# Attention and fp8 linear layer on one core: k projected in natural order, mask constants as 32 rows

## What is computed

```python
xn = _layernorm(x, axis=-1)
x = x + attn(xn, q_w, k_w, v_w, o_w, o_b, unity_scale) \
      + ffn(xn, weight_fp8, bias, input_scale, weight_scale)

# attn
allowed = (j % STRIDE == 0) | (jnp.abs(i - j) <= LOCAL)      # STRIDE = 4, LOCAL = 8
q = (x @ q_w) * sigmoid(unity_scale);  k = x @ k_w;  v = x @ v_w     # by heads
scores = jnp.einsum('bhqd,bhkd->bhqk', q, k) / sqrt(D)
attn = softmax(jnp.where(allowed, scores, -jnp.inf))
out = einsum('bhqk,bhkd->bhqd', attn, v) @ o_w + o_b
# ffn
x_dq = clip(x / input_scale, -448, 448).astype(float8_e4m3fn).astype(x.dtype) * input_scale
out = einsum('bsi,oi->bso', x_dq, weight_fp8 * weight_scale) + bias
```

## Time and profile before

| | us |
|---|---|
| median of 3 runs | 1383.69 |
| their range | 1381.85 to 1384.70 |
| profiled execution, its own time | 1381.62 |
| its span | 1379.8 |
| TensorE busy | 1270.9 (92%) |
| VectorE busy | 1019.7 (74%) |
| ScalarE busy | 841.5 (61%) |
| POOL busy | 264.0 (19%) |

### The profile page before, as it was taken

The page is one execution under the profiler, slowest core; times in us unless marked ns, Lnnn a source line. Parts: engine busy times, 40 slices in busy tenths (PEclk is TensorE's granted clock), DMA queues, the critical chain, the costliest instruction groups (busy, mean ns, idle before and its releaser), DMA issues.

```text
span 1379.8 us, 28508 instructions
## 1 busy us (share of the span) xinstructions
PE 1270.9 (92%) x9536; PEld 600.6 (44%) x9536; DVE 1019.7 (74%) x2567; ACT 841.5 (61%) x1540; POOL 264.0 (19%) x381
## 2 busy tenths in 40 slices
PE   5279999954999999999999999999999999999996
PEld 3166767621443433334343433443344334334385
DVE  4299999754887878878887887888788878888232
ACT  2144555411777777777776776777677777777800
POOL 2043333320112111211211122111211121121200
PEclk9689999975999999999999999999999999999999
DMA  3268778962244545354443535354454535442257
GB/s 113 78 183 228 230 219 232 212 192 45 59 106 108 116 107 110 110 112 105 106 114 100 117 100 119 95 121 102 99 116 110 110 99 121 107 107 93 77 192 284
DMA packets 207965, 177.82 MB, mean 129 GB/s; under 512 B 48774, under 2 KB 185046, under 8 KB 206230
## 3 DMA queue, kind: packets, MB, share of 16 engines
q1 hardware_dynamic: 201296, 168.84, 47.9%
q10 hardware_dynamic: 6528, 7.08, 1.6%
HBM read 106.78 MB, written 68.29 MB: 127 GB/s over the span
## 4 chain that ended last, share of the span: by engine, by line
PE 66%; DVE 7%; DMA 3%; issue 1%; ACT 1%; SPq 0%; ACTq 0%; DVEq 0%
PE ps_attend L969 19%; PE ps_attend L954 18%; PE ps_attend L932 15%; DVE masked L900 7%; PE ps_attend L976 5%; PE ps_attend L1062 3%; PE ps_attend L955 3%; PE ps_attend L938 2%; DMA q_op<-q_parts_dram 2%; DMA q_op<-attn_dram 1%; PE ps_attend L929 1%; ACT probs L849 0%; SPq L83 0%; SPq L756 0%; ACT probs L854 0%
## 5 line engine op out<-in xcount | busy, mean ns | idle before, releaser
L900 DVE CUSTOM_DVE_ANT_0 masked<-ps_attend,max_mask 128x620 bf16<-128x620 f32 x1024 | 773.9, 798 | 216.1 <-PE ps_attend L955 208.4
L849 ACT ACTIVATE probs<-ps_attend 128x512 f32<-128x512 f32 x1024 | 563.4, 599 | 212.2 <-PE ps_attend L932 189.8
L954 PE MATMUL ps_attend<-k_op,q_op 96*128 96x512 bf16 x1024 | 398.4, 396 | 35.5 <-DMA q_op<-q_parts_dram 21.1
L932 PE MATMUL ps_attend<-q_op,k_op 99*128 99x512 bf16 x1024 | 309.9, 383 | 10.4 <-issue 9.4
L969 PE MATMUL ps_attend<-probs,v_op 128*32 128x512 f32 x2048 | 275.1, 609 | 0.2 <-ACT probs L849 0.2
L954 PEld LDWEIGHTS ps_attend<-k_op,q_op 96*128 96x128 bf16 x1024 | 99.0, 97 | 331.6 <-DVE peak L900 250.6
L955 PE MATMUL ps_attend<-k_op,q_op 96*128 96x108 bf16 x1024 | 219.3, 214 | 0.0
L730 POOL CAST negmax<-peak 128x16 bf16<-128x16 f32 x64 | 12.6, 196 | 809.2 <-DVE peak L900 809.2
L932 PEld LDWEIGHTS ps_attend<-q_op,k_op 99*128 99x128 bf16 x1024 | 84.7, 98 | 148.9 <-ACT probs L849 49.0
L854 ACT ACTIVATE probs<-ps_attend 108x512 f32<-108x512 f32 x256 | 146.5, 601 | 0.7 <-PE ps_attend L938 0.7
L955 PEld LDWEIGHTS ps_attend<-k_op,q_op 96*128 96x128 bf16 x1024 | 102.0, 100 | 16.6 <-issue 0.8
(11 more groups left out here) (67 smaller groups left out, 969.8 us busy)
## 6 DMA issues: line engine op xcount, KB each, us to landing
k_op<-k_parts_dram SPq DMA_DIRECT2D x96, 256.0 KB, 5.0
q_op<-q_parts_dram SPq DMA_DIRECT2D x384, 64.0 KB, 2.7
v_dram<-v_sb SPq DMA_DIRECT2D x64, 256.0 KB, 3.1
share_rows<-shares_dram SPq DMA_DIRECT2D x64, 256.0 KB
attn_dram<-out_rows SPq DMA_DIRECT2D x64, 256.0 KB, 4.2
v_op<-v_dram SPq DMA_DIRECT2D x48, 288.0 KB
q_parts_dram<-qk_parts SPq DMA_DIRECT2D x48, 256.0 KB, 3.8
k_parts_dram<-qk_parts SPq DMA_DIRECT2D x48, 192.0 KB, 2.3
```

The lines of the kernel that those rows point to most:

```text
L849: ins = nc.scalar.activation(probs[:, r, h], ps_s[st.bank(kind)], ACT.Exp)
L900: nc.vector.tensor_tensor_reduce(masked[:, i % 2], ps_u[i % 2][:, 0:UNIT], keep["max_mask"][:, mask], 1.0, -3e38, ALU.add, ALU.max, peak[: ...
L932: ins = nc.tensor.matmul(bank, k[0:KM, h * S + r * P:h * S + (r + 1) * P], q[0:KM, h], start=True, stop=True)
L954: nc.tensor.matmul(ps_u[i % 2][:, 0:NS], cols, k[0:KR, h * S:h * S + NS], start=True, stop=True)
```

## The change

k is projected in natural order: one matmul of 512 columns in place of one of 128 and one of 384. ScalarE's copy of k and VectorE's first subtraction for k read the bank with a stride and write in the order that attention wants, each as two instructions (`in_order` and `by_stride` give the two views). The constants are 32 rows in DRAM: the three rows of -1 (of zeros on q's side, overwritten by the maxima later) stand ahead of the 29. So POOL's two memsets and their semaphores go, and ScalarE waits at the start of attention until the rows of `q_op` have landed, since it writes maxima over three of them.

```diff
+        def in_order(keys):
+            keys = keys.rearrange("p i (g r) -> p i g r", r=STRIDE)
+            return keys[:, :, :, 0], keys[:, :, :, 1:]
+        def by_stride(keys):
+            ns = CH // STRIDE
+            return keys[:, :, 0:ns], keys[:, :, ns:].rearrange("p i (g r) -> p i g r", r=STRIDE - 1)
...
-            sp.dma_start(keep["k_op"][KM:P], io["near_k"].bitcast(BF16)).then_inc(keep["bands_loaded"], 16)
+            sp.dma_start(keep["k_op"][KR:P], io["near_k"].bitcast(BF16)).then_inc(keep["bands_loaded"], 16)
             for slot in range(QSLOTS):
-                sp.dma_start(keep["q_op"][KM:P, slot], io["near_q"].bitcast(BF16)[:, slot * CH:(slot + 1) * CH].unsqueeze(1)
-                             .broadcast_to([P - KM, HG, CH])).then_inc(keep["bands_loaded"], 16)
+                sp.dma_start(keep["q_op"][KR:P, slot], io["near_q"].bitcast(BF16)[:, slot * CH:(slot + 1) * CH].unsqueeze(1)
+                             .broadcast_to([P - KR, HG, CH])).then_inc(keep["bands_loaded"], 16)
...
-                if isinstance(c, int) and c == 1:
-                    pool.wait_ge(y8_ready, 2)
-                    nc.gpsimd.memset(keep["k_op"][KR:KM], -1.0).then_inc(ones_set, 1)
-                    pool.wait_ge(ones_set, 1)
...
-                    nc.scalar.activation(qk_parts[:, k, 1, 0], ps_k, ACT.Copy).then_inc(hi_ready, 1)
+                    for to, src in zip(by_stride(qk_parts[:, k, 1, 0]), in_order(ps_k)):
+                        last = nc.scalar.activation(to, src, ACT.Copy)
+                    last.then_inc(hi_ready, 1)
...
-                nc.vector.tensor_tensor(rest[:, w], src, qk_parts[:, k, w, 0], ALU.subtract).then_inc(rest_ready, 1)
+                if w == 0:
+                    last = nc.vector.tensor_tensor(rest[:, w], src, qk_parts[:, k, w, 0], ALU.subtract)
+                else:
+                    for to, of, hi in zip(by_stride(rest[:, w]), in_order(src), by_stride(qk_parts[:, k, w, 0])):
+                        last = nc.vector.tensor_tensor(to, of, hi, ALU.subtract)
+                last.then_inc(rest_ready, 1)
...
-                        for cols, keys in ((slice(0, ns), grouped[:, :, :, 0]), (slice(ns, CH), grouped[:, :, :, 1:])):
-                            for i in range(KC):
-                                last = nc.tensor.matmul(ps_k[:, m, cols], wk[:, i, m * P:(m + 1) * P], keys[:, i],
-                                                        start=(i == 0), stop=(i == KC - 1))
+                        for i in range(KC):
+                            last = nc.tensor.matmul(ps_k[:, m], wk[:, i, m * P:(m + 1) * P], xnT[:, k, i],
+                                                    start=(i == 0), stop=(i == KC - 1))
...
             pool.wait_ge(tails_set, 2)
-            nc.gpsimd.memset(k_op[1][KR:KM], -1.0).then_inc(ones_set, 1)
-            pool.wait_ge(ones_set, 1)
...
-            sp.dma_start(k_op[1][KM:P], io["near_k"].bitcast(BF16)).then_inc(keep["bands_loaded"], 16)
+            sp.dma_start(k_op[1][KR:P], io["near_k"].bitcast(BF16)).then_inc(keep["bands_loaded"], 16)
...
+            act.wait_ge(keep["bands_loaded"], 16 * (QSLOTS + 1))
             unrolled(body)
...
-                    if st.n == 1:
-                        pe.wait_ge(ones_set, 1)
```

More of the change, by code:

```diff
@@ L133, in part_project @@
         masks_ready = sem("masks_ready")
-        ones_set = sem("first_ones_set")
         zeros_set = sem("zeros_set")
@@ L504, in body @@
                         pe.wait_ge(rest_ready, 2 * c)
-                    grouped = xnT[:, k].rearrange("p i (g r) -> p i g r", r=STRIDE)
-                    ns = CH // STRIDE
                     for m in range(KC):
-                        for cols, keys in ((slice(0, ns), grouped[:, :, :, 0]), (slice(ns, CH), grouped[:, :, :, 1:])):
-                            for i in range(KC):
-                                last = nc.tensor.matmul(ps_k[:, m, cols], wk[:, i, m * P:(m + 1) * P], keys[:, i],
-                                                        start=(i == 0), stop=(i == KC - 1))
+                        for i in range(KC):
+                            last = nc.tensor.matmul(ps_k[:, m], wk[:, i, m * P:(m + 1) * P], xnT[:, k, i],
+                                                    start=(i == 0), stop=(i == KC - 1))
                     last.then_inc(k_ready, 1)
@@ L659, in part_attend @@
         tails_set = sem("tails_set")
-        ones_set = sem("ones_set")
         q_loaded = keep["q_loaded"]
@@ L1125 @@
     close = np.abs(STRIDE * (place // 3) + 1 + place % 3 - np.arange(S)[:, None]) <= LOCAL
-    near_q = np.where(rows.astype(int) @ close.T.astype(int), np.float32(0), np.float32(-BIG))
-    near_k = np.zeros((P - KM, HG * S + KTAIL), np.float32)
+    near_q = np.zeros((P - KR, S), np.float32)
+    near_q[PARTS:] = np.where(rows.astype(int) @ close.T.astype(int), 0, -BIG)
+    near_k = np.zeros((P - KR, HG * S + KTAIL), np.float32)
+    near_k[:PARTS] = -1
     for h in range(HG):
-        near_k[:, h * S + NS:(h + 1) * S] = rows[:, WPAD:-WPAD]
-        near_k[:, h * S + NS - WPAD:h * S + NS] = 1
+        near_k[PARTS:, h * S + NS:(h + 1) * S] = rows[:, WPAD:-WPAD]
+        near_k[PARTS:, h * S + NS - WPAD:h * S + NS] = 1
     for h in range(HG + 1):
-        near_k[:, h * S:h * S + WPAD] = 1
+        near_k[PARTS:, h * S:h * S + WPAD] = 1
     def bf16_bits(a):
```

## The result

| | before | after |
|---|---|---|
| median (4 runs each, taken together) | 1383.81 | 1351.61 |
| their range | 1381.85 to 1384.70 | 1350.56 to 1354.34 |
| profiled execution, its own time | 1381.62 | 1354.34 |
| its span | 1379.8 | 1352.5 |

The ratio is 0.9772, 95% interval 0.9754 to 0.979: 2.3% faster, 32.2 us where 59.4 were forecast. 1351.61 lies well above the range of 1318 to 1333. The profiled executions differ by 27.3 us; before's was 2.2 under its median, after's the slowest of its four and 2.7 over.

What follows compares the result with a forecast made beforehand. TensorE was taken as busy except in two stalls behind 29-row mask loads on one DMA engine, with an equally long POOL, ScalarE and VectorE loop in projection. 33.2 + 5.5 - 1.0 + 1.0 - 0.3 + 21.0 = 59.4 us gave 1324, range 1318 to 1333.

Steps and rivals of the forecast that it cites:

- whose steps stay as they are: Attention: the gap of 21 us goes and the steps there do not change.
- C: Rival: strided bank reads run at half rate, the cut of k grows 1.1 us in 15 chunks: 1341, chance 0.06.
- D: Rival: strided reads severely slow, at five times the time per element the cut adds 4.5 us x 15: 1392, chance 0.01.
- Mask rows, first place: Start of the kernel: 32 rows spread over sixteen DMA engines, so the third x lands earlier: 33.2 us gained.
- B: Rival: only `k_op`'s long rows spread, `q_op`'s stay on one engine, some 14 us lost: 1338, chance 0.05.
- E: Rival: the change spreads nothing, one DMA engine moves a tenth more: 1384, no change, chance 0.03.
- The memset: Second chunk: without POOL's fill of three rows VectorE's clamp no longer takes 6.18 us: 5.5 us gained.
- POOL's wait for the copy of q: Second chunk: POOL's second operation waits for the copy of q: 1.0 us lost.
- The +1.0 of the long chunk of before: Projection: one chunk of 15.03 us, where TensorE, slow after stalls, made POOL wait, shortens: 1.0 us back.
- Natural order: Projection: TensorE gains 0.97 us per chunk, hidden by another loop; the split cut of k makes chunks 14.03 us: 0.3 us lost.
- A: Rival: TensorE's 0.97 us per chunk counts in full, 14 chunks x 1.0 us: 1310, chance 0.04.
- Mask rows, second place: Start of attention: the first six q loads land earlier behind the mask rows, TensorE's idle time goes: 21.0 us gained.

Runs made afterwards that it cites:

- e3: The changed kernel with k projected, copied and cut as before, so only the 32 mask rows and no POOL memsets: 1328.46 us.
- e5: The changed kernel with TensorE's attention loop aligned to the start of a 256-instruction block: 1328.73 us.
- e8: e5 with the third x loaded ahead of `max_mask` and the mask rows: 1325.74 us.
- e7: e5 with k projected, copied and cut as in the kernel before: 1329.01 us.
- e6: The changed kernel with TensorE's attention loop aligned to slot 216 of its 256-instruction block, 40 instructions left: 1336.40 us.
- e1: The changed kernel with 192 more TensorE instructions, waits for a count long reached, ahead of attention: 1345.99 us.
- e2: The kernel before with 64 more TensorE instructions, waits for a count long reached, ahead of attention: 1407.08 us.

## Why the prediction was wrong

The direction was right. The size was wrong by 27.6 us in the median. One step accounts for most of it: e3 and e5, in which the jumps cost what they cost before, are 23 us faster than the changed kernel. The other 5 us are sizes of terms in the first two places.

**The step that failed** is in the prediction's last part: no gap in attention, "whose steps stay as they are". It followed the operations that the change touches and gave no term to what the change does to the place of all the code behind them. The plain steps did stay, at 14.98 us. The jumps did not: +27.7 us between the profiled executions, of which before's lies 2.2 us under its median and after's 2.7 over, so some 23 us between the medians. Part of this could be seen in the kernel before, if not in the earlier trace rows: six steps there are 1.7 to 3.6 us longer, with TensorE idle for "issue". The prediction did not look at them. That they hung on a position in the program no row of before shows. The rivals had none of this kind either; C and D looked for a loss from natural order in the cut of k, where there was none.

**Mask rows, first place**, 33.2 forecast, 28.6 measured. The rows did spread, and B and E fell. Mis-sized was the time at which x lands: 23 us by the 335 GB/s of the earlier trace rows, 30.4 measured, at 134 to 184 GB/s. The 0.6 us for k of the first chunk lay under this wait. In e8, where it doesn't, 25.20 to 38.63 is 13.4 us, against 13.2 forecast.

**The memset**, 5.5 forecast, 5.6 measured: from the second chunk to the third the gain grows from 28.6 to 34.2. VectorE's clamp is back at its 0.69 us:

```profile
49.03 0.69 DVE L429 TENSOR_SCALAR quant<-quant 128x1024 f32<-128x1024 f32 x1 [0.70 <-ACT quant L322]
```

**POOL's wait for the copy of q**, -1.0, came one chunk later than forecast, as 0.87 us in the row at 60.23, because x was late; in e8 it is in its place (53.84 - 38.63 = 15.2). The +1.0 of the long chunk of before is the growth from 33.5 to 34.5.

**Natural order.** Right. Chunks 14.02 us for 14.03 forecast. The cut's two pieces in the kernel after, by form (busy us, mean ns):

```profile
L421 DVE TENSOR_TENSOR rest<-ps_project,qk_parts 128x768 f32<-128x768 f32 x12 | 11.4, 948 | 0.0
...
L421 DVE TENSOR_TENSOR rest<-ps_project,qk_parts 128x256 f32<-128x256 f32 x12 | 5.1, 424 | 0.0
```

These are 0.42 and 0.95 us, and the two together take 1.29 in place of 1.23. That is no more than the 0.08 us for a second instruction, so the strided read costs nothing that shows, and C falls. The reason for which the prediction took this lower end was a wrong reading, though: it has VectorE at twice TensorE's time per element, and its own rows give 1.04 ns against 0.83 (275 ns for 128 columns, 592 for 512). That the lower end was the right one is luck as far as it rests on this. TensorE has its time back and waits with it:

```profile
185.20 1.06 PE L509 MATMUL ps_project<-ident,xn 128*128 128x128 f32 x8 [0.86 <-DVE base L357]
...
186.10 3.60 PE L518 MATMUL ps_project<-xnT,wk 128*128 128x512 f32 x8
```

k takes 3.60 us, and TensorE idles for some 0.86 us in each chunk; 3.60 and 0.9 were forecast. So A falls.

**Mask rows, second place**, 21.0 forecast, 19.4 measured: the first six q loads came 1.6 us late, for which the range had allowed.

Together they make 53.9 us at the second step, 5.5 short: x makes 4.6 of it and the q loads 1.6, and small terms give 0.7 back. e3, e5 and e7, in which the jumps cost as before, give 1328 to 1329: inside the range and some 5 us over the forecast, as the 5.5 say.

## What to carry over

An edit that removes instructions from an engine moves every loop behind them in that engine's program. A turn of this loop of TensorE cost some 2 or 3 us, or some 7, depending on where its start landed: look at the steps around each jump back, and at "issue" rows, before and after, and align, hint or unroll such a loop before weighing the edit itself. An edit that looks bad in the total should be run with the loop's place held fixed; here natural order changed from 25 us slower to nothing. Loads that are spread over all DMA engines need not run at the rate that other loads reached (here 134 to 184 GB/s in place of 335), so put what someone waits for ahead of such loads.

## What the runs showed of the hardware

- A turn of TensorE's loop cost 1.6 to 4.1 us with 84 or 256 instructions left in its block, 3.7 to 6.3 with 40 (e6), and 5.5 to 8.9 with 20. With the hint it was at most 0.5, unrolled nothing. By the rule of the Trainium skill (Runtime: NRT & Kernel Launch, section "Instruction fetch mechanics") the waits are fetches; the runs show that position decides, and no row shows the fetch itself.
- At each jump of the changed kernel, with its two waits, TensorE then ran at 1.2 GHz for some 7 to 14 us (an estimate from the mean clock in stretches of 4 us), and about half of what a jump cost was lost in that time. Whether a single wait pulls the clock down varies from turn to turn in the same kernel (1.8 and 3.2 us before); what decides that stays open.
- An instruction of TensorE that waits for a count already reached took 0.11 to 0.12 us (e1, e2).
- While the loads of 32 rows ran, the DMA engines had a share of 1.0 and moved 134 to 184 GB/s. Whether the few partitions, the source repeated for four heads, or the loads that ran beside them set that rate was not tried.
- VectorE's read of a bank with a stride of four columns, or three of four, cost no more per element than an adjacent one (0.42 and 0.95 us for 256 and 768 elements, 1.23 for 1024 adjacent ones).
